# A Mamba block and a feed-forward block on one core: another order of steps on each engine

## The reference

```
x = x + layernorm(mamba2(layernorm(x)))
x = x + layernorm(ffn(layernorm(x)))

mamba2(u): zxbcdt = u @ in_proj                      # 256 -> 512 z, 512 x, 128 B, 128 C, 8 dt
           xBC = silu(causal_conv1d(xBC, 4 taps) + bias)
           dt = softplus(dt + dt_bias);  dA = dt * -exp(A_log)
           state[t] = exp(dA[t]) * state[t-1] + B[t] (x) (x[t] * dt[t])     # 8 heads, 64 x 128 each
           y = C[t] . state[t] + x * D
           y = rmsnorm(y * silu(z)) * norm_weight;  return y @ out_proj
ffn(x):    W = lut[4-bit codes] * scales             # gate, up: 2048 x 256; down: 256 x 2048
           return (gelu_tanh(x @ Wg.T) * (x @ Wu.T)) @ Wd.T
```

## Time and profile before

| | |
|---|---|
| median of three executions | 1031.8 us |
| profiled execution | 1033.27 us, its span 1031.5 us |
| TensorE matmul busy | 935.3 us (91%) |
| VectorE busy | 821.9 us (80%) |
| ScalarE busy | 574.2 us (56%) |
| GpSimd busy | 357.5 us (35%) |
| chain that ended last | TensorE 80%, VectorE 10%, ScalarE 5%, issue 4% |
| TensorE's granted clock, mean | 0.966 of full speed |

### The profile page before, as it was taken

How to read it: one execution, slowest core, us unless ns; L and a number is a source line. 1 busy time by engine, 2 the same in 40 slices (tenths; PEclk the granted TensorE clock), 3 DMA queues, 4 the chain that set the end, 5 groups by cost and what they waited for, 6 DMA issues and landing times.

```text
span 1031.5 us, 17892 instructions
## 1 busy us (share of the span) xinstructions
PE 935.3 (91%) x5984; PEld 805.4 (78%) x5984; DVE 821.9 (80%) x2135; ACT 574.2 (56%) x935; POOL 357.5 (35%) x349
## 2 busy tenths in 40 slices
...
DMA packets 13845, 17.82 MB, mean 17 GB/s; under 512 B 1712, under 2 KB 10416, under 8 KB 13744
## 3 DMA queue, kind: packets, MB, share of 16 engines
...
q10 hardware_dynamic: 864, 0.03, 0.1%
...
## 4 chain that ended last, share of the span: by engine, by line
PE 80%; DVE 10%; ACT 5%; issue 4%; POOL 1%; DMA 0%; ACTq 0%; POOLq 0%; DVEq 0%
PE fb L1070 33%; PE db L1070 16%; PE mb L1070 14%; PE mb L1194 5%; PE mb L1203 3%; PE mb L1185 2%; DVE lmat L840 2%; PE mb L1209 1%; PE mb L1150 1%; ACT L691 1%; PE mb L1177 1%; DVE xc L866 1%; DVE stage L1033 1%; ACT xc L651 1%; PE mb L1112 1%
## 5 line engine op out<-in xcount | busy, mean ns | idle before, releaser
L562 POOL TENSOR_TENSOR hl<-hid,hl 128x512 fp32r<-128x512 f32 (+1 forms) x144 | 178.4, 1240 | 435.1 <-ACT hl L698 435.1
L1070 PE MATMUL fb<-x1t,wg 128*128 128x512 f32 (+1 forms) x864 | 216.5, 386 | 8.7 <-issue 4.6
L1070 PE MATMUL db<-wd,hl 128*128 128x256 f32 x1536 | 210.2, 286 | 3.6 <-POOL hl L562 3.6
L1070 PE MATMUL fb<-x1t,wu 128*128 128x512 f32 (+1 forms) x864 | 204.3, 372 | 3.2 <-ACT hid L691 2.4
L1070 PEld LDWEIGHTS db<-wd,hl 128*128 128x128 f32 x1536 | 192.1, 188 | 15.0 <-issue 8.4
L1070 PEld LDWEIGHTS fb<-x1t,wu 128*128 128x128 f32 x864 | 150.8, 189 | 36.9 <-ACT hid L691 6.6
L1070 PEld LDWEIGHTS fb<-x1t,wg 128*128 128x128 f32 x864 | 145.5, 189 | 41.9 <-issue 13.1
L974 DVE TENSOR_TENSOR hid<-fb,hid 128x512 f32<-128x512 f32 (+1 forms) x144 | 90.5, 628 | 67.0 <-PE fb L1070 62.4
L698 ACT ACTIVATE hl<-hid 128x512 fp32r<-128x512 f32 (+1 forms) x144 | 83.7, 581 | 96.2 <-DVE hid L974 73.1
L866 DVE SCALAR_TENSOR_TENSOR xc<-raw,cw,xc 128x256 f32<-128x256 f32 x288 | 118.8, 482 | 15.0 <-ACT xc L651 13.9
L691 ACT ACTIVATE hid<-fb 128x512 f32<-128x512 f32 (+1 forms) x144 | 78.8, 548 | 82.8 <-PE fb L1070 74.8
...
## 6 DMA issues: line engine op xcount, KB each, us to landing
...
cb<-in_conv_b ACTq DMA_DIRECT2D x1, 3.0 KB, 3.6
```

Of the source, the lines that this page charges most:

```text
L562: pool.tensor_tensor(hl[:, hs, n % 2, 1, :], hid[:, hs, n % 2, :], hl[:, hs, n % 2, 0, :].bitcast(F32), ALU.subtract).then_inc(s["lo"], 1)
L1070: last = pe.matmul(ps, lhs(a, k), rhs(b, k), start=start and n == 0, stop=stop and n == len(todo) - 1, skip_group_check=check)
```

## The change

The lists `ORDER` and `FIRST` are written in another order for all four engines. Each list holds the same steps as before. Since the banks follow from `ORDER["pe"]`, eight Mamba steps wait for another reader: dt:1 for yt:1's (was ip:3's), ip:4 for ip:3's (was yt:1's), ip:5 for dt:1's, z:2 for ip:4's, and at the end of a block dt_t:0 for dt:0's, ip:1 for out:3's, z:0 for ip:1's and z:1 for dt_t:0's. Of `FIRST` the opening of ScalarE's and VectorE's lists is shown, and TensorE's whole.

```diff
--- before.py
+++ after.py
@@ -65,82 +65,80 @@
 
 ORDER = {
     "pe": """
-        gu:0< cs:0 gu:1< gu:2< dn:0< dn:1< ct:0 gu:3< seg:0 seg:1 seg:2 dn:2< xtr:0 gu:4< gb:0 seg:3 yo:0
-        gu:5< dn:3< yd:0 st:0 gu:6< yt:0 dn:4< xtr:1 out:0 yo:1 yd:1 dn:5< dn:6< st:1 xt:1 gu:7< yt:1 ip:3
-        gu:8< out:1 dn:7< ip:4 dt:1 gu:9< dt_t:1 gu:10< dn:8< ip:5 dn:9< z:2 cs:1 z:3 gu:11< ct:1 seg:4
-        seg:5 gu:12< seg:6 seg:7 gb:1 dn:10< yo:2 xtr:2 xt:0> gu:13< yd:2 st:2 dn:11< yt:2 dn:12< xtr:3
-        out:2 yo:3 yd:3 gu:14< st:3 dn:13< yt:3 gu:15< out:3 dn:14< x1t:0 dt:0> dn:15< ip:0> dt_t:0> ip:1>
-        ip:2> x1t:1 z:0> z:1>""",
+        gu:0< gu:1< cs:0 gu:2< dn:0< gu:3< dn:1< ct:0 seg:0 seg:1 dn:2< seg:2 xtr:0 gu:4< gb:0 seg:3 yo:0 gu:5<
+        dn:3< yd:0 st:0 gu:6< yt:0 xtr:1 dn:4< out:0 yo:1 dn:5< dn:6< yd:1 st:1 xt:1 gu:7< yt:1 ip:3 gu:8< out:1
+        dt:1 ip:4 gu:9< dn:7< dt_t:1 ip:5 gu:10< z:2 dn:8< cs:1 gu:11< z:3 ct:1 seg:4 gu:12< seg:5 seg:6 dn:9<
+        seg:7 gb:1 dn:10< yo:2 xtr:2 xt:0> gu:13< yd:2 dn:11< st:2 yt:2 xtr:3 dn:12< out:2 yo:3 gu:14< yd:3 st:3
+        dn:13< yt:3 gu:15< out:3 x1t:0 dt:0> dn:14< dn:15< ip:0> ip:1> dt_t:0> x1t:1 ip:2> z:0> z:1>""",
     "act": """
-        silu:0 gelu:0< gelu:1< split:0< split:1< gelu:2< silu:1 gate:0 gate:1 split:2< silu:2 exps:0 gelu:3<
-        decay_matrix:0 decay_matrix:1 decay_matrix:2 split:3< gelu:4< decay_matrix:3 gb_copy:0 split:4<
-        gelu:5< square:0 split:5< yt_split:0 gelu:6< split:6< xn_split:1 square:1 gelu:7< yt_split:1
-        split:7< taps:3 gelu:8< silu:3 split:8< dt_copy:1 taps:4 gelu:9< gelu:10< split:9< dt_bias:1 taps:5
-        silu:4 gate:2 silu:5 gate:3 split:10< gelu:11< decay_matrix:4 exps:1 decay_matrix:5 decay_matrix:6
-        decay_matrix:7 gb_copy:1 split:11< gelu:12< split:12< gelu:13< xn_split:0> square:2 yt_split:2
-        split:13< gelu:14< square:3 yt_split:3 split:14< gelu:15< split:15< x1_split:0 dt_copy:0> taps:0>
-        dt_bias:0> x1_split:1 taps:1> taps:2>""",
+        silu:0 gelu:0< gelu:1< split:0< split:1< gelu:2< silu:1 split:2< gate:0 gate:1 gelu:3< silu:2
+        decay_matrix:0 decay_matrix:1 exps:0 decay_matrix:2 split:3< gelu:4< decay_matrix:3 gb_copy:0 split:4<
+        gelu:5< square:0 split:5< yt_split:0 gelu:6< split:6< xn_split:1 gelu:7< square:1 yt_split:1 split:7<
+        taps:3 gelu:8< split:8< dt_copy:1 gelu:9< silu:3 taps:4 dt_bias:1 gelu:10< split:9< taps:5 gate:2
+        split:10< silu:4 gelu:11< gate:3 silu:5 exps:1 decay_matrix:4 split:11< decay_matrix:5 decay_matrix:6
+        decay_matrix:7 gb_copy:1 gelu:12< xn_split:0> split:12< gelu:13< square:2 split:13< yt_split:2 gelu:14<
+        square:3 yt_split:3 gelu:15< split:14< split:15< x1_split:0 dt_copy:0> taps:0> taps:1> x1_split:1
+        dt_bias:0> taps:2>""",
     "dve": """
-        conv:1 inter:0< inter:1< decays:0 conv:2 inter:2< stats1:1 sums:0 decay_sums:0 decay_sums:1
-        decay_sums:2 xdt:0 inter:3< xn:1 decay_sums:3 gb_copy:0 decayed_products:0 yoff:0 inter:4<
-        decayed_products:1 ydiag:0 state:0 inter:5< yt_split:0 inter:6< xdt:1 stats2:0 yoff:1 ln2:0 state:1
-        ydiag:1 xn_split:1 x1n:0 inter:7< yt_split:1 conv:3 stats2:1 inter:8< ln2:1 conv:4 dt_bias:1
-        inter:9< inter:10< stats1:0> x1n:1 softplus:1 conv:5 decays:1 xn:0> sums:1 decay_sums:4 decay_sums:5
-        inter:11< decay_sums:6 decay_sums:7 gb_copy:1 decayed_products:2 xdt:2 yoff:2 inter:12<
-        decayed_products:3 inter:13< xn_split:0> ydiag:2 state:2 yt_split:2 xdt:3 stats2:2 yoff:3 ln2:2
-        ydiag:3 state:3 inter:14< yt_split:3 inter:15< stats2:3 x1n:2 ln2:3 fin:0< x1_split:0 x1n:3
-        dt_bias:0> conv:0> softplus:0> x1_split:1 ln4:0<""",
+        inter:0< conv:1 inter:1< decays:0 inter:2< conv:2 sums:0 decay_sums:0 inter:3< decay_sums:1 decay_sums:2
+        xdt:0 stats1:1 gb_copy:0 decay_sums:3 decayed_products:0 xn:1 yoff:0 inter:4< decayed_products:1 ydiag:0
+        inter:5< state:0 yt_split:0 inter:6< xdt:1 stats2:0 yoff:1 ln2:0 state:1 ydiag:1 xn_split:1 inter:7<
+        yt_split:1 inter:8< stats2:1 conv:3 ln2:1 inter:9< x1n:0 dt_bias:1 conv:4 softplus:1 inter:10< stats1:0>
+        decays:1 xn:0> conv:5 sums:1 inter:11< decay_sums:4 decay_sums:5 decay_sums:6 x1n:1 decay_sums:7
+        gb_copy:1 decayed_products:2 xdt:2 inter:12< yoff:2 inter:13< xn_split:0> ydiag:2 decayed_products:3
+        state:2 yt_split:2 xdt:3 stats2:2 yoff:3 ln2:2 ydiag:3 inter:14< yt_split:3 state:3 inter:15< stats2:3
+        x1n:2 ln2:3 fin:0< x1n:3 x1_split:0 dt_bias:0> conv:0> x1_split:1 softplus:0> ln4:0<""",
     "pool": """
-        split:0< split:1< split:2< stats1:1 xdt:0 split:3< yoff:0 split:4< split:5< split:6< stats2:0 xdt:1
-        yoff:1 ln2:0 split:7< stats2:1 split:8< ln2:1 split:9< stats1:0> split:10< split:11< xdt:2 yoff:2
-        split:12< split:13< xdt:3 stats2:2 yoff:3 ln2:2 split:14< split:15< stats2:3 ln2:3 fin:0<""",
+        split:0< split:1< split:2< xdt:0 stats1:1 split:3< yoff:0 split:4< split:5< split:6< stats2:0 xdt:1
+        yoff:1 ln2:0 split:7< split:8< stats2:1 ln2:1 split:9< stats1:0> split:10< split:11< xdt:2 yoff:2
+        split:12< split:13< stats2:2 xdt:3 yoff:3 ln2:2 split:14< split:15< stats2:3 ln2:3 fin:0<""",
 }
 
 FIRST = {
     "pe": """
-        xt:1 ip:3 ip:4 dt:1 dt_t:1 ip:5 z:2 cs:1 z:3 ct:1 seg:4 seg:5 seg:6 seg:7 gb:1 yo:2 xtr:2 xt:0> yd:2
-        st:2 yt:2 xtr:3 out:2 yo:3 yd:3 st:3 yt:3 out:3 dt:0> ip:0> dt_t:0> ip:1> ip:2> z:0> x1t:1 z:1> gu:0
-        cs:0> ct:0> seg:0> seg:1> gu:1 seg:2> dn:0 gb:0> xtr:0> seg:3> gu:2 yo:0> gu:3 yd:0> st:0> dn:1 dn:2
-        yt:0> xtr:1> gu:4 dn:3 gu:5 out:0> yo:1> yd:1> xt:1> gu:6 dn:4 st:1> dn:5 yt:1> gu:7 gu:8 dn:6 ip:3>
-        out:1> dt:1> ip:4> gu:9 gu:10 dt_t:1> gu:11 ip:5> z:2> cs:1> z:3> dn:7 ct:1> seg:4> seg:5> dn:8 dn:9
-        seg:6> dn:10 seg:7> gb:1> yo:2> xtr:2> gu:12 gu:13 xt:0>> yd:2> st:2> dn:11 yt:2> gu:14 xtr:3> out:2>
-        yo:3> dn:12 yd:3> gu:15 x1t:0> yt:3> dn:13 st:3> out:3> dt:0>> ip:0>> dn:14 dn:15 dt_t:0>> ip:1>> ip:2>>
-        x1t:1> z:0>> z:1>>""",
+        xt:1 ip:3 dt:1 ip:4 dt_t:1 ip:5 z:2 cs:1 z:3 ct:1 seg:4 seg:5 seg:6 gb:1 seg:7 yo:2 xtr:2 xt:0> yd:2
+        st:2 yt:2 xtr:3 out:2 yo:3 yd:3 st:3 yt:3 out:3 dt:0> ip:0> dt_t:0> ip:1> x1t:1 ip:2> z:0> z:1> cs:0>
+        gu:0 ct:0> seg:0> seg:1> gu:1 seg:2> dn:0 gb:0> xtr:0> seg:3> gu:2 yo:0> gu:3 yd:0> st:0> dn:1 dn:2
+        yt:0> xtr:1> gu:4 dn:3 gu:5 out:0> yo:1> yd:1> xt:1> gu:6 st:1> dn:4 dn:5 yt:1> gu:7 gu:8 dn:6 ip:3>
+        out:1> dt:1> ip:4> gu:9 gu:10 dn:7 dt_t:1> ip:5> z:2> z:3> cs:1> ct:1> seg:4> seg:5> gu:11 dn:8 dn:9
+        seg:6> seg:7> dn:10 gb:1> yo:2> xtr:2> gu:12 gu:13 xt:0>> yd:2> st:2> dn:11 yt:2> gu:14 xtr:3> out:2>
+        yo:3> dn:12 yd:3> gu:15 dn:13 yt:3> st:3> x1t:0> out:3> dn:14 dt:0>> ip:0>> ip:1>> dt_t:0>> ip:2>>
+        x1t:1> dn:15 z:0>> z:1>>""",
     "act": """
-        xn_split:1 wi_split:0 wi_z:0 wo_split:0 dl:0 dl:1 taps:3 dt_copy:1 rates:0 dt_bias:1 dl:2 taps:4 taps:5
-        silu:3 silu:4 dl:3 gate:2 gate:3 exps:1 silu:5 decay_matrix:4 dl:4 decay_matrix:5 decay_matrix:6
-        decay_matrix:7 gb_copy:1 dl:5 xn_split:0> square:2 dl:6 yt_split:2 dl:7 dl:8 square:3 dl:9 yt_split:3
-        dl:10 dt_copy:0> dl:11 taps:0> dt_bias:0> taps:1> x1_split:1 taps:2> gate:0> gate:1> silu:0> gelu:0
+        rates:0 xn_split:1 wi_split:0 wi_z:0 wo_split:0 dl:0 dl:1 taps:3 dt_copy:1 dl:2 dt_bias:1 taps:4 taps:5
+        dl:3 gate:2 silu:3 gate:3 silu:4 silu:5 decay_matrix:4 exps:1 decay_matrix:5 dl:4 decay_matrix:6
+        decay_matrix:7 gb_copy:1 dl:5 xn_split:0> dl:6 square:2 yt_split:2 dl:7 dl:8 square:3 dl:9 yt_split:3
+        dt_copy:0> dl:10 dl:11 taps:0> taps:1> x1_split:1 dt_bias:0> taps:2> gate:0> gate:1> silu:0> gelu:0
...
     "dve": """
-        stats1:1 xn:1 wi_split:0 dq:0 scale:0 dq:1 wo_split:0 stats1:0> scale:1 xn:0> xn_split:1 wo_lo:0 dl:1
-        dl:0 dq:2 dt_bias:1 scale:2 rates:0 softplus:1 conv:3 dq:3 conv:4 scale:3 decays:1 dq:4 sums:1 dl:2
-        conv:5 decay_sums:4 dl:3 dq:5 decay_sums:5 scale:4 gb_copy:1 decay_sums:6 decay_sums:7 scale:5
-        decayed_products:2 dq:6 xdt:2 yoff:2 dl:4 dl:5 scale:6 ydiag:2 state:2 decayed_products:3 dq:7
-        xn_split:0> scale:7 dl:6 dq:8 xdt:3 yt_split:2 scale:8 dq:9 yoff:3 dl:8 scale:9 stats2:2 dl:7 ydiag:3
-        dq:10 ln2:2 scale:10 state:3 yt_split:3 dq:11 stats2:3 scale:11 ln2:3 x1n:2 dt_bias:0> conv:0> x1n:3
-        softplus:0> x1_split:1 conv:1> decays:0> conv:2> inter:0 sums:0> decay_sums:0> decay_sums:1>
...
+        stats1:1 xn:1 rates:0 wi_split:0 dq:0 wo_split:0 scale:0 dq:1 stats1:0> scale:1 xn:0> xn_split:1 wo_lo:0
+        dl:1 dq:2 dl:0 scale:2 dq:3 dt_bias:1 conv:3 scale:3 softplus:1 dl:2 conv:4 decays:1 conv:5 sums:1
+        decay_sums:4 decay_sums:5 dl:3 dq:4 gb_copy:1 dq:5 decay_sums:6 scale:4 decay_sums:7 decayed_products:2
```

(8 more changed lines are left out.)

29 lines of the change are left out of this document (13 added, 16 removed).

## The result

The kernel after took 1025.8 us (median of four executions, 1024.4 to 1026.3), the kernel before beside it 1032.0: a ratio of 0.9928, 95% interval 0.9913 to 0.9943. (The two medians alone give 0.9940.) Forecast were 1024.5 us and faster. The profiled execution took 1025.26 us with a span of 1023.5, 8.0 less than before's 1031.5.

A forecast was written before the change was run, and what follows sets the result against it. Bounds: VectorE to 122 us, both near full to 209, then TensorE in the loop. Terms -4.1 + 1.0 - 1.1 - 0.5 - 1.8 - 2.3 = -8.8, plus 1.5 reserve: -7.3, giving 1024.5 us; range 1019 to 1031.5.

The forecast's parts named there:

- z:1's wait: End of a block on TensorE: the new order removes z:1's 0.69 us idle, six times, -4.1 us.
- Head of the block: Start of each loop block: thin ScalarE slack (0.3 us) may make gu:1 wait, +1.0 us; VectorE's slack 0.85 us.
- hidden 0.18: Third gate of a block: 0.18 us of waiting inside TensorE's busy time goes, six times, -1.1 us.
- What follows what: TensorE's loop: fewer costly changes to a three-pass group, 22 instead of 25, -1.8 us, bounds 0 and -2.5.
- Table load: ScalarE's loop, ahead of gelu:10: one more load of 1.28 us a block, taken to cost 0.
- The start: Before 122 us: rates:0 delays VectorE +3.3, covered waits -6.4, ydiag:3 +0.8; sum -2.3, bounds +3.3 and -3.1.
- The block from 122 to 209: Block between start and loop: same work done by seg:6 in both orders, 0 us, bounds -2 and +2.
- rival C: Loop: TensorE's waits only move and changed step sequence saves nothing, leaving the start's gain; 1030.5 us, chance 0.16.
- my reserve of 1.5: Loop: +1.5 us for small waits in seven blocks from steps followed only by their neighbours.
- Rival B: Start: the 3.3 us are lost and gaps come again elsewhere; about 1027.8 us, or 1026 to 1030, chance 0.16.
- D: ScalarE's tail in every block: late chain makes gu:1 wait, kernel slower, 1036.4 us at 2.0 us late; chance 0.10.
- E: Whole kernel better: ydiag:3 finds its add done, block heads cost nothing, no small waits; about 1020.5 us, chance 0.05.

The follow-up runs named there:

- e5: Kernel after with ScalarE's loop tail in its old order (dt_bias:0 ahead of x1_split:1 and taps:1): 1032.53 us, ratio 0.9996 to before.
- e6: Kernel after with conv:1 again ahead of inter:0 in VectorE's loop list: 1030.02 us, ratio 0.9969 to before.
- e1: Kernel after with rates:0 back in its old place in FIRST on ScalarE and VectorE: 1022.96 us, ratio 0.9900 to before.
- e4: Kernel after with xtr:0 one step later in TensorE's loop, behind gu:4: 1026.19 us, ratio 0.9934 to before.
- e7: Kernel after with both conv:1 ahead of inter:0 and rates:0 in its old place: 1027.23 us, ratio 0.9943 to before.
- e9: e1 with the loop over blocks 2 to 7 written out on TensorE alone: 1022.17 us, ratio 0.9887 to before.
- e10: e1 with ln4 cut in two, its subtractions later, conv:1 ahead of inter:0, VectorE's blocks 2 to 7 written out: 1018.63 us, ratio 0.9845 to before.
- e12: e10 with the loop written out also on TensorE, ScalarE and GpSimd: 1015.93 us, ratio 0.9827 to before.
- e11: e10 with the loop written out on TensorE too: 1017.25 us, ratio 0.9839 to before.

## Why the prediction was right, step by step

The direction, the size and the range held. The forecast span was 1024.2 (-7.3), the measured 1023.5; but two errors of some 5 us each cancel in it, and some 1.2 us of the gain ahead of block 2 go with the clock, not with the order (point 7). That the number is so close is luck.

1. *z:1's wait*, -4.1: right, six of six. e5 shows that with the new banks it is ScalarE's tail order that keeps TensorE from waiting here.
2. *Head of the block*: ScalarE's tail chain cost nothing (gelu:0 ends at 553.34, the up group that needs it starts at 553.52: a slack of 0.2 us, 0.3 by the count); the +1.0 was not needed. VectorE's slack I had counted only to x1_split:1, and not behind it: with softplus:0 moved there, inter:0 would come some 1.5 us later against gu:0 than before. So inter:0 ahead of conv:1 is worth far more than the "hidden 0.18": without it e6 waits 1.10 us in a block without a jump.
3. *What follows what*, -1.8: not isolated. From block 2 to block 8, before's listed waits and the slow stretch below are 4.1 + 4.6 + 0.5 + 1.5 = 10.7 us, after's are 1.4 + 1.0 + 0.5 + 0.4 + 0.2 and six of the seven xtr:0, 5.0, together 8.5. That is 2.2 of the 3.9; 1.7 is left for this and the hidden wait, against 2.9 forecast.
4. *Table load*, 0: TensorE doesn't wait near gelu:10 in the loop.
5. and 6. *The start*, -2.3: the first inter comes at 119.21, 3.0 us earlier. rates:0 cost its 3.3 (e1: 3.5 at the same place), the six waits went, and ydiag:3 found its add done (GpSimd took 1.26 us for it, not 2.24), so the lower bound was the right value. A wait I had not listed took some of it: 1.0 us ahead of scale:2, which the waits view puts down to no engine; by the kernel it waits for its scales from DMA.
7. *The block from 122 to 209*, 0: measured -1.7, and most of that is not the order. z:3 waits 2.1 us and ct:1 1.7, close to the 1.9 and 1.4 forecast. VectorE's 1.30 and 0.49 us at gb:0 and xtr:0 in this block are gone; but in before they are waits for TensorE, at 126 to 128 us, and TensorE's granted clock was at the lower of its two levels (1.2 GHz, 0.50 of full speed) just then, for twice as long as in after. Windows view of before, then of after (length, TensorE's busy time, clock):

```profile
121.20:128.00 6.80, 5.08 (x26) 0.50 0.01 1
```

```profile
116.30:119.70 3.40, 3.13 (x20) 0.50 0.00 0
```

Of the ten traces with after's `FIRST`, with or without rates:0 put back, five have the clock at 0.50 until 5.1 to 6.1 us behind the first inter (e4, e7, e9, e10, e12) and take 86.6 to 86.8 us from there to block 2; the five where it is back within 1.3 us (after, e1, e5, e6, e11) take 85.5. So 1.2 us go with the long stretch at the low clock. Before has such a stretch and takes 87.3, so its like is e4 with 86.6, and the order gave some 0.6 us here. The five traces with the long stretch are also those in which block 2 starts late for their `FIRST`.

What failed is the sentence "the two issue gaps are at the jump back of the loop; the change leaves the loop as it is, so they stay". They fell by 3.2 us. And behind the gap of 2.55 us before's clock was low, by the windows view in the same columns:

```profile
441.80:446.30 4.50, 4.49 (x13) 0.62 0.39 122
446.30:450.00 3.70, 3.70 (x19) 1.00 0.00 0
```

A gate and an up group took 4.4 us there in place of 2.9; after has no such place. Behind the second gap, of 2.06 us, the clock was 1.00; so one gap in before cost this and the other did not. Against this gain of 4.7 stands the new wait at xtr:0, 5.8 us in seven blocks. That was rival C's mechanism (a wait moved), though at a step that neither C nor my reserve of 1.5 had named: I followed VectorE's order at the head of the block to inter:0 and conv:1, but not what conv then runs beside. Rival B is excluded by the first inter, 3.0 us earlier, and by block 2's start, and D by the absence of any wait on `hid` L689 in the loop. Of E two conditions held (ydiag:3, step 2), the third, no small waits, did not. (Two of the rivals' sums are a little off: E's three terms, 0.8, 1.0 and 1.5, give 1021.2 and not 1020.5, and B's 1027.8 is 3.3 above mine, not 3.) The loop's period is 0.7 us shorter a block, where the prediction's sign was about 1 us.
